# A state space layer with routed experts: GpSimd's input product for all four channel tiles of a state in one instruction

## What is computed

```python
xg = xn @ in_proj_w
x_inner, gate = jnp.split(xg, 2, axis=-1)
x_inner = x_inner * jax.nn.silu(gate)
xc = conv over 4 taps of x_inner            # shortened
dt = jax.nn.softplus(xc @ dt_w + dt_b)      # 512 inner channels
A_bar = jnp.exp(dt[..., None] * A)          # 16 states for each channel
B_bar = dt[..., None] * Bm[:, :, None, :]
def step(h, inp):
    a_t, b_t, xc_t, c_t = inp
    h = a_t * h + b_t * xc_t[..., None]
    y = jnp.einsum('bds,bs->bd', h, c_t) + D_skip * xc_t
    return (h, y)
```

## Time and profile before

| | us |
|---|---|
| median of 3 executions | 1931.46 (1931.4 to 1935.31) |
| profiled execution | 1939.45 |
| its span, first to last instruction | 1937.8 |
| busy: PE, DVE | 1524.1, 1256.9 |
| busy: ACT, POOL | 778.9, 1016.0 |

### The profile page before, as it was taken

One profiled execution on the slowest core, in us unless ns is written; L12 is line 12 of the kernel. 1 busy time (PEld: TensorE's weight loads), 2 busy tenths in 40 slices (PEclk: granted clock), 3 DMA queues, 4 the chain that ended last, 5 costly groups with the idle time before them and its releaser, 6 DMA issues. The chain is left out here.

```text
span 1937.8 us, 22792 instructions
## 1 busy us (share of the span) xinstructions
PE 1524.1 (79%) x6572; PEld 996.6 (51%) x6572; DVE 1256.9 (65%) x2109; ACT 778.9 (40%) x1378; POOL 1016.0 (52%) x1238
## 2 busy tenths in 40 slices
PE   5787888888887888878876665699999999999600
PEld 2344545545544445445445443467777777777400
DVE  1399999999999999998999962112222222222266
ACT  3555456466465566474563432112211222212122
POOL 0669678788688698687787744011111111111274
PEclk9898899999999999999997597799999999999855
DMA  3111121121122012111111101661101111111165
GB/s 90 50 33 47 42 55 47 58 60 52 53 56 71 27 61 76 39 55 60 46 48 60 49 33 62 222 229 34 33 31 33 32 33 33 33 33 33 41 194 174
DMA packets 78326, 122.22 MB, mean 63 GB/s; under 512 B 12256, under 2 KB 47936, under 8 KB 78208
## 3 DMA queue, kind: packets, MB, share of 16 engines
q1 hardware_dynamic: 60640, 80.12, 13.5%
q0 software_dynamic: 13344, 36.46, 5.9%
q10 hardware_dynamic: 4224, 4.19, 0.6%
HBM read 89.15 MB, written 31.59 MB: 62 GB/s over the span
## 5 line engine op out<-in xcount | busy, mean ns | idle before, releaser
L856 POOL TENSOR_TENSOR bb<-u,br 128x512 f32<-128x512 f32 x512 | 647.6, 1273 | 204.5 <-DVE hh L707 202.9
L591 ACT ACTIVATE bA<-dt,a_neg 128x512 f32<-128x512 f32 x512 | 351.5, 690 | 448.3 <-DVE hh L707 447.6
L466 PE MATMUL bH<-ident,hh 128*128 128x128 f32 x2048 | 344.1, 296 | 166.6 <-DVE hh L707 116.5
L466 PEld LDWEIGHTS bH<-ident,hh 128*128 128x128 f32 x2048 | 259.5, 151 | 412.3 <-DVE hh L707 180.0
L724 DVE SCALAR_TENSOR_TENSOR yT<-bH,bc,yT 128x512 f32<-128x512 f32 x480 | 348.4, 726 | 17.6 <-PE bH L466 17.0
L707 DVE TENSOR_TENSOR_SCAN hh<-bA,hl,bb 128x512 f32<-128x512 f32 x256 | 325.4, 1271 | 1.1 <-ACT bA L591 1.1
L707 DVE TENSOR_TENSOR_SCAN hh<-bA,bb 128x512 f32<-128x512 f32 x256 | 309.2, 1209 | 25.0 <-ACT bA L591 15.9
L1249 POOL DMA_DIRECT2D expert_out_scratch<-yt x71 | 38.7, 544 | 481.7 <-DVE yt L1331 472.5
L1120 PE MATMUL bD<-w_d,hT 128*128 x852 | 197.6, 382 | 0.8 <-ACT hT L1291 0.8
L1285 ACT ACTIVATE sgm<-bG 128x352 f32<-128x352 f32 x142 | 58.1, 461 | 325.6 <-PE bG L1077 325.6
L1077 PE MATMUL bG<-w_g,xtT 128*128 x568 | 181.9, 463 | 1.9 <-DMA w_d<-in_L_ffn_Wd_dram 1.3
(11 more groups left out here) (185 smaller groups left out, 1861.2 us busy)
## 6 DMA issues: line engine op xcount, KB each, us to landing
br<-b_scratch SPq DMA_DIRECT2D x128, 256.0 KB, 3.2
xt<-expert_in_scratch POOLq DMA_DIRECT2D x71, 128.0 KB, 2.3
expert_out_scratch<-yt POOLq DMA_DIRECT2D x71, 128.0 KB, 2.0
w_g<-in_L_ffn_Wg_dram SPq DMA_DIRECT2D x8, 704.0 KB, 4.3
w_u<-in_L_ffn_Wu_dram SPq DMA_DIRECT2D x8, 704.0 KB, 5.9
w_d<-in_L_ffn_Wd_dram SPq DMA_DIRECT2D x8, 640.0 KB, 7.0
xp<-in_L_attn_x_dram SPq DMA_DIRECT2D x8, 512.0 KB, 5.0
xr<-in_L_attn_x_dram SPq DMA_DIRECT2D x8, 512.0 KB, 5.0
```

Source lines behind the costliest of these rows:

```text
L466: i = e.transpose(bH[g % NH][:, q * P:(q + 1) * P], hh[:, (n - 1) % 2, q, d * P:(d + 1) * P], ident[:])
L591: e.activation(bA[g % NA][:], dt[c % 2][:, d, :], ACT.Exp, scale=a_neg[:, d, n:n + 1]).then_inc(s_a, 1)
L856: e.tensor_tensor(bb[:, k % NB, :], u[c % 2][:, d, :], br[:, n % NR, :], ALU.mult).then_inc(s_bb, 1)
```

## The change

GpSimd's product of input and B row was one instruction for each slot. It becomes one instruction for each state: 128 partitions by 4 tiles by 512 tokens, with the B row read four times through a broadcast view. `bb` has two buffers of four tiles instead of four of one. The product of state n+1 is issued in slot 4n, ahead of the other steps of that slot, and waits until all four scans of state n-1 are done. It waits for the inputs u of all four tiles at once where it waited for one. `s_bb` now counts states: VectorE waits for it only at the first slot of a state, and the two other places that use the count, the B row's load and ScalarE's reuse of u, are put in the same unit.

```diff
@@ constants
-AHEAD_ACT, AHEAD_POOL, AHEAD_ROW = NA - 1, 3, 12
-NR = NB = 4
+AHEAD_ACT, AHEAD_ROW = NA - 1, 12
+NR, NB = 4, 2
@@ phase1
-        bb = sb("bb", [P, NB, CH])
+        bb = sb("bb", [P, NB, ND, CH])
@@ sp_row
-            used = c * SLOTS + (n - NR) * ND + ND
+            used = c * NS + n - NR + 1
@@ act_proj
-                        e.wait_ge(s_bb, SLOTS * (c - 1))
+                        e.wait_ge(s_bb, NS * (c - 1))
@@ dve_scan
-            e.wait_ge(s_bb, g + 1)
+            if d == 0:
+                e.wait_ge(s_bb, g // ND + 1)
...
-            e.tensor_tensor_scan(hh[:, n % 2, d, :], bA[g % NA][:], bb[:, k % NB, :], hl[:, n, d:d + 1] if c % 2 else 0.0,
+            e.tensor_tensor_scan(hh[:, n % 2, d, :], bA[g % NA][:], bb[:, n % NB, d, :], hl[:, n, d:d + 1] if c % 2 else 0.0,
                                  ALU.mult, ALU.add).then_inc(s_scan, 1)
@@ pool_input
-        def pool_input(e, c, k):
-            n, d = divmod(k, ND)
-            g = c * SLOTS + k
+        def pool_input(e, c, n):
+            g = c * NS + n
             if n == 0:
-                e.wait_ge(s_u, ND * c + d + 1)
-            if d == 0:
-                e.wait_ge(s_bl[n % NR], 16 * (NS // NR * c + n // NR + 1))
+                e.wait_ge(s_u, ND * (c + 1))
+            e.wait_ge(s_bl[n % NR], 16 * (g // NR + 1))
             if g >= NB:
-                e.wait_ge(s_scan, g - NB + 1)
-            e.tensor_tensor(bb[:, k % NB, :], u[c % 2][:, d, :], br[:, n % NR, :], ALU.mult).then_inc(s_bb, 1)
+                e.wait_ge(s_scan, ND * (g - NB + 1))
+            e.tensor_tensor(bb[:, n % NB, :, :], u[c % 2][:], br[:, n % NR, :].unsqueeze(1).broadcast_to([P, ND, CH]), ALU.mult).then_inc(s_bb, 1)
@@ pool_main
-            if k + AHEAD_POOL < SLOTS:
-                pool_input(e, c, k + AHEAD_POOL)
-            elif c + 1 < NCH:
-                pool_input(e, c + 1, k + AHEAD_POOL - SLOTS)
+            if k % ND == 0:
+                n = k // ND + 1
+                if n < NS:
+                    pool_input(e, c, n)
+                elif c + 1 < NCH:
+                    pool_input(e, c + 1, 0)
@@ gpsimd queue, before the first chunk
-                    for k in range(AHEAD_POOL):
-                        pool_input(e, 0, k)
+                    pool_input(e, 0, 0)
```

## The result

Over 8 executions of each kernel the changed one has a median of 1945.14 us, the one before 1934.72 us: ratio 1.0044, 95% interval 1.0026 to 1.0062. A second group of runs gave 1945.8 against 1937.16 us, 1.0043 (1.0028 to 1.0058). The change makes the kernel 0.4% slower.

A forecast was written before the change was run, and what follows sets the result against it. VectorE was taken to bound the scan stretch. Terms 1.8 + 10.0 - 3.6 - 1.7 + 0.5 + 4.0 = +11.0 us on the median 1931.46 gave 1942.5 us, range 1932 to 1955.

The forecast's parts named there:

- Product: GpSimd's product over 2048 elements: 4.52 us, extrapolated from 512 and 1024; the saving itself, off the path, worth nothing.
- Rival A: GpSimd's long product takes 5.09 us: +22.8 us, 1954.3 us; chance 0.18 with what lies between.
- Start: First scan waits for four tiles at once, starting by 81.85 us instead of 80.06: +1.8 us.
- Compares: VectorE's one-hot compares in slot 56 wait for whole GpSimd instructions: 23.4 us instead of 13.4, +10.0 us.
- Rival B: In slot 56 the second compare keeps its turn when the product ends: -0.4 us, 1931.1 us; chance 0.12.
- hl: VectorE's waits for GpSimd's last-column copy shrink: -3.6 us at three even-chunk starts, -1.7 us in three smaller waits.
- States 10 and 11: In the three later even chunks, GpSimd's full queue may delay hl by 0.1 us per state: put at +0.5 us.
- a sign of being wrong: ScalarE or TensorE waits appearing in states held covered would show the forecast wrong; no size given.
- TensorE: Late mm_ in slot 58 lengthens TensorE's wait and may lower its clock in four more chunks: +4 us, bounds 0 and 8.
- short waits of 0.3 us stand: TensorE waits in slots 10 to 20; the faster rival, 1927.5 us, chance 0.07, needed them not to become the wait.

The follow-up runs named there:

- r2: Changed kernel, the two compares reading logits from PSUM and moved from slot 56 to 55: 1935.44 us, 0.9986 of before.
- r4: Changed kernel, GpSimd making mm_ in slot 56 straight behind the product, ahead of the dt sum and u product: 1932.76 us, 0.9974 of before.
- r1: The changed kernel run again with no edit: 1945.8 us.
- r6: Changed kernel, each state's product as four back-to-back instructions of 128x512 with the same queue place and gates: 1953.21 us in one execution.
- r5: Changed kernel, the two compares of a chunk as one instruction of 128x64: 1937.77 us in one execution, before beside it 1936.54.
- r3: Kernel before, with the compares reading logits from PSUM in slot 55: 1930.21 us, 0.9965 of before.
- r10: Kernel before, compares from PSUM in slot 54 and mm_ made in slot 55: 1915.99 us, 0.9948 of before.
- r9: Changed kernel, compares from PSUM in slot 54 and mm_ in slot 55, ahead of the long product: 1909.53 us, 0.9905 of before.
- r8: Changed kernel, the hl copy moved ahead of the product in the next state's first slot: 1941.92 us in one execution.
- r11: Changed kernel, compares from PSUM in slot 54, mm_ in slot 55, hl copy ahead of the product: 1906.23 us, 0.9884 of before.
- r12: Kernel before, compares from PSUM in slot 54, mm_ in slot 55, hl copy at the next state's start: 1903.26 us, 0.9871 of before.
- r7: Changed kernel, only the very first state's product split in four, each released by itself: scan stretch 1062.6 us in one execution, changed 1057.0.

## Why the prediction was right, point by point

**The time.** 1942.5 us was forecast with 1932 to 1955, and 1945.14 measured. The forecast was +11.0 us on a median of 1931.46; measured were +10.4 on 1934.72, the median of before over more executions, so the 2.6 us between the two times come from the start value. The parts of the stretch came out like this:

- **Product**, 4.52 us: 4.539. The line through 512 and 1024 elements holds at 2048 with a broadcast operand. Rival A (5.09) falls. The Trainium skill (GPSIMD Engine Reference, Performance versus the Vector engine) gives 4497 ns for an add of this size; the trace has 4539 ns, 1% more, for this multiply.
- **Start**, +1.8: +2.3. The first product began at 77.77 us instead of 77.20, which is the other half microsecond; it ended 4.5 us later as reckoned.
- **Compares**, +10.0 (23.4 us): +10.5 (23.9 us), with pairs of 3.55 to 3.6 us and a last one of 2.42. r2 shows that they wait for the other engine, r4 that the second loses its turn to the instruction that GpSimd has ready (in 21 of 24 pairs, see r1), r6 that they pay for its length. In one pair of before the first compare lost its turn too, and twice (2.94 us at 990.10 us, chunk 6), so who goes next is the usual outcome and no law. Rival B falls with the 3.55 us above; r4 is what B would have been. One thing in this term was not sound. It puts the 10 us "all on VectorE's path". But where VectorE waits in slot 59, its compares and the wait for mm_ cover each other: r2 keeps 8.9 of 21.9 us, r5 none of 7.2, and r1 in chunk 4 none of 1.1. The late mm_ is as much the loss as the compares are.
- **hl**, -5.3: -5.4. Three waits of 1.29, 1.13 and 1.10 us were left where 1.1 were expected, and the three small ones are gone. The wait before scan 8 of chunk 4 is still there:

```profile
623.98 0.21 POOL L869 COPY hl<-hh 128x4 f32<-128x4 f32 x1
...
624.32 1.22 DVE L708 TENSOR_TENSOR_SCAN hh<-bA,bb 128x512 f32<-128x512 f32 x1 [1.13 <-POOL hl L869]
```

- **States 10 and 11**, +0.5: no wait there. ScalarE: its waits for va2 appear (15.4 us in 7 pieces) and cost VectorE nothing: it has no wait in slots 19 to 33. VectorE's waits for the decay in slot 16 of chunks 2, 4 and 6 are new, 0.45 us each; with two small ones gone that is +1.0 us, where the prediction had nothing and named such a wait as a sign of being wrong. Their cause was not looked for.
- **TensorE**, +4: wrong in its sum, right in its place. In slots 58 to 60 VectorE's waits grew by 5.9 us (2.8 to 8.7), within its bounds of 0 and 8. In the others they fell by 7.4 (14.5 to 7.1), which the prediction did not have. Together -1.5 us where +4 stood.

TensorE's timeline in slot 58 and 59 of chunk 3, where nothing was lost before (answering to rows 9):

```profile
592.30 0.65 PE L428 MATMUL A<-mm_,below 128*128 128x40 f32 x2 [3.34 <-POOL mm_ L818]
...
596.30 1.06 PE L466 MATMUL bH<-ident,hh 128*128 128x128 f32 x4
...
598.48 0.60 PE L466 MATMUL bH<-ident,hh 128*128 128x128 f32 x4
```

And the changed kernel's stretches around it (busy us of PE, PEld, DVE, ACT, POOL with counts; then the granted clock, the DMA share and GB/s):

```profile
592.50:597.00 4.50, 4.50 (x16) 3.36 (x17) 3.11 (x4) 4.45 (x8) 1.22 (x1) 0.50 0.31 105
598.50:602.00 3.50, 2.98 (x21) 2.25 (x20) 3.50 (x6) 2.94 (x6) 2.45 (x4) 1.00 0.11 39
```

After the wait of 3.34 us for mm_ TensorE runs at a granted clock of 0.50, that is 1.2 GHz, for the ranking, the shared expert's matmuls and the transposes. VectorE then waits 1.79 us in slot 59. That part of the term was as forecast: 1.8 us each in chunks 3 and 5, where there was no wait in slots 58 to 60 before, and 2.3 us instead of 0.7 in chunk 4.

The term's failed half is the slots behind hl. Before, the even chunks 2, 4 and 6 had waits of 0.18 to 1.38 us in slots 11 to 14 behind each hl wait of over 2 us, 4.8 us in sum. With hl waits of 1.1 us the changed kernel has none there. I had held them for TensorE's own load ("short waits of 0.3 us stand") and so thought they would limit the gain. In the other runs the two mostly go together. With hl waits of over 2.3 us these waits stand in 6 of 9 chunks (3 of 3 before, 1 of 3 in r3, 2 of 3 in r10). With hl waits of 1.1 to 1.3 us they stand in 1 of 21 (r9, 1.9 us in chunk 2), and in r6, r8, r11 and r12, with hl waits of about 2 us or none, in none. So the long hl wait makes them likely but not sure; by which way (a lower clock after it, or the order of the queues) was not separated. The other 2.6 us of the 7.4 are mostly in slots 16 to 18 of the odd chunks and in slot 4 of chunk 0, and they are not explained.

**How it adds up.** Compares +10.5, hl -5.4, TensorE +5.9 and -7.4, ScalarE +1.0 give +4.6 us, against 3.6 measured for the stretch; with the start 6.9 against 5.9. The 1.0 us between them is not accounted for. The profiled executions differ by 5.3 us in time, the medians by 10.4. The profiled execution of before lay 4.7 us above its median, that of after at it. So the forecast of the median was lucky in part: its +11 us held 5.5 us too much for TensorE, while the median moved 5 us more than the profiles. What the executions without a profile do otherwise stays open. The part behind the last scan varies by more than that (794 to 806 us over all profiles), but there is no trace of these executions to show it there.

## What to carry to other kernels

An engine that is not the bound can still lengthen instructions of the one that is. Look for short VectorE instructions with a mean far above their size (996 ns for 32 elements was the sign), see whether their ends fall on the ends of GpSimd's instructions, and give them a PSUM operand or put GpSimd into a wait there before you make GpSimd's instructions longer. When such a wait is taken away, ask who is late next: here the tile for TensorE's ranking had to move ahead in GpSimd's queue as well, or the gain came back in the next slots.

## What the runs showed of the hardware

A compare of two SBUF operands, 128x32, took 1745 ns in the mean beside GpSimd products of 4.54 us, 878 ns beside products of 1.27 us in the same queue, and 189 ns with one operand in PSUM. Between two such instructions of VectorE, GpSimd's next one came first in 21 of 24 cases where it was ready (changed kernel, r1, r7, r8). The scans, whose tensor operands are one in PSUM and one in SBUF, took 1209 ns beside either product. And shortening instructions of the bounding engine did not shorten the stretch: r5 took 7.2 us out of the compares and was 3.1 us longer, since VectorE's wait behind them for TensorE grew by 8.8. TensorE, after waiting 3.34 us for its operand, ran at a granted clock of 0.50 there, and four transposes took 1.06 us instead of 0.60.
